# Layer-norm normalisations moved from VectorE to ScalarE in a two-layer model kernel, with new orders on four engines

## The reference: what is computed

```python
h = _L0_tok_ref(x, L0_tok_W, L0_tok_b)
h = jnp.concatenate([h, txt], axis=1)
h = h + _L0_attn_ref(_layernorm(h, axis=-1))          # plain attention, no projections
h = h + _L0_ffn_ref(_layernorm(h, axis=-1), ...)      # router takes the better half of the tokens, gelu
h = h + _L1_attn_ref(_layernorm(h, axis=-1), ...)     # 16 query heads, 1 key head, rotary, window 128
h = h + _L1_ffn_ref(_layernorm(h, axis=-1), ...)      # 32 experts, the best one for each token, relu

def _layernorm(x, axis=-1, eps=1e-05):
    m = jnp.mean(x, axis=axis, keepdims=True)
    v = jnp.var(x, axis=axis, keepdims=True)
    return (x - m) / jnp.sqrt(v + eps)
```

## Time and profile before

| | |
|---|---|
| median of three runs | 582.66 us (579.9 to 582.99) |
| the profiled execution | 583.62 us, its span in the trace 581.8 us, mean granted clock 0.971 |
| PE busy | 502.2 us (86%) |
| weight loads of PE | 386.4 us (66%) |
| DVE busy | 417.8 us (72%) |
| ScalarE busy | 311.9 us (54%) |
| GpSimd busy | 234.7 us (40%) |
| starts of hC | 148.97, 209.70, 270.42, 332.37, 394.34, 452.97, 508.66, 556.86 us |

### The profile page before, as it was taken

How to read it: one execution, slowest core, us unless ns; L and a number is a source line. 1 busy time by engine, 2 the same in 40 slices (tenths; PEclk the granted TensorE clock), 3 DMA queues, 4 the chain that set the end, 5 groups by cost and what they waited for, 6 DMA issues and landing times.

```text
span 581.8 us, 14569 instructions
## 1 busy us (share of the span) xinstructions
PE 502.2 (86%) x5920; PEld 386.4 (66%) x5920; DVE 417.8 (72%) x1291; ACT 311.9 (54%) x593; POOL 234.7 (40%) x217
## 2 busy tenths in 40 slices
PE   3457499879999899989998999899989999899845
PEld 2235277658867786778776877688767767777622
DVE  3669766996799769976997699957995697363220
ACT  1414346565667556766577565756575655454311
POOL 2316632554446342643454436354462446420000
PEclk9999999989999999999998999899999999999966
DMA  7000000000000000000000000000000000000000
GB/s 271 1 6 0 1 7 2 3 1 7 3 2 10 7 2 2 10 7 3 2 9 3 2 3 2 8 3 2 3 10 2 2 2 9 2 3 9 2 1 7
DMA packets 6450, 6.29 MB, mean 11 GB/s; under 512 B 4208, under 2 KB 5744, under 8 KB 6256
## 3 DMA queue, kind: packets, MB, share of 16 engines
q1 hardware_dynamic: 6384, 5.37, 3.0%
HBM read 4.31 MB, written 0.79 MB: 9 GB/s over the span
## 4 chain that ended last, share of the span: by engine, by line
PE 47%; DVE 35%; ACT 9%; POOL 2%; issue 2%; DMA 2%; SPq 1%; POOLq 0%; ACTq 0%; DVEq 0%
PE bank L961 38%; PE bank L979 10%; DVE eq L515 5%; DVE negm L631 4%; DVE q_sb L568 4%; DVE ssq L585 4%; DVE tb L568 4%; DVE on L648 3%; ACT qT L810 3%; POOL qs L793 2%; DMA p<-masks 2%; DVE eq L506 1%; ACT qs L810 1%; DVE eq L431 1%; DVE rec L644 1%
## 5 line engine op out<-in xcount | busy, mean ns | idle before, releaser
L631 DVE TENSOR_REDUCE negm<-bank 128x2 f32<-128x384 f32 (+1 forms) x128 | 79.2, 619 | 39.6 <-PE bank L961 38.4
L793 POOL TENSOR_TENSOR qs<-q_sb,qs 128x1024 fp32r<-128x1024 f32 x24 | 56.8, 2368 | 107.8 <-ACT qs L810 107.8
L919 ACT ACTIVATE p<-bank 128x512 f32<-128x512 f32 x112 | 66.0, 599 | 56.6 <-PE bank L961 55.4
L961 PE MATMUL bank<-kh,qT 128*128 128x128 f32 (+1 forms) x384 | 82.0, 323 | 0.0
L810 ACT ACTIVATE qT<-bank 128x512 fp32r<-128x512 f32 x96 | 54.3, 596 | 50.3 <-PE bank L979 49.9
L961 PE MATMUL bank<-vx,p 128*64 128x65 f32 x1536 | 68.8, 225 | 1.3 <-DVE on L648 1.2
L961 PEld LDWEIGHTS bank<-vx,p 128*64 128x64 f32 x1536 | 60.5, 138 | 13.9 <-issue 6.8
L756 POOL TENSOR_TENSOR q_sb<-q_sb,tb 128x512 f32<-128x512 f32 x24 | 36.5, 1519 | 74.3 <-DVE tb L568 74.3
L961 PEld LDWEIGHTS bank<-kh,qT 128*128 128x128 f32 x384 | 64.2, 199 | 2.1
L961 PE MATMUL bank<-sh_r,sh_l 128*128 128x512 f32 x112 | 53.2, 475 | 0.0
L644 DVE RECIPROCAL rec<-bank 128x4 f32<-128x4 f32 (+1 forms) x88 | 15.7, 179 | 48.4 <-PE bank L961 48.0
(11 more groups left out here) (158 smaller groups left out, 1122.9 us busy)
## 6 DMA issues: line engine op xcount, KB each, us to landing
wts<-weights SPq DMA_DIRECT2D x1, 1313.5 KB, 7.3
h<-txt SPq DMA_DIRECT2D x1, 672.0 KB, 8.4
img<-images SPq DMA_DIRECT2D x8, 72.0 KB, 1.9
q_sb<-wqkv SPq DMA_DIRECT2D x1, 576.0 KB, 9.7
sh_r<-mT SPq DMA_DIRECT2D x32, 4.0 KB
out<-o_sb SPq DMA_DIRECT2D x8, 64.0 KB, 1.9
p<-masks SPq DMA_DIRECT2D x1, 480.0 KB, 10.4
cst<-shapes SPq DMA_DIRECT2D x1, 304.0 KB, 3.8
```

The costliest lines, as they stand in the source:

```text
L631: ve.tensor_reduce(dst, src, AX_X, ALU.max, negate=True).then_inc(s_vec, 1)
L793: gp.tensor_tensor(qs[:, :, D:2 * D], ta[:, t, 0:NH, :], qs[:, :, 0:D].bitcast(F32), ALU.subtract).then_inc(b_pool, 1)
L919: ac.activation(dst.rearrange("s h t -> s (h t)"), bank[BANK_E[n % 2]][:, :], ACT.Exp).then_inc(e_act, 1)
L961: return pe.matmul(dst, lhsT, rhs, start=start, stop=stop, skip_group_check=True)
```

## The change

Nine of the eleven instructions of DVE that normalise A's two norms and D's norm become ScalarE activations (Identity, scale column `rs`, bias column `nm`), since (x - m) r = r x + (-m r). The two that write `xpad` stay on DVE, and so does B's norm. GpSimd makes the bias: it negates the means ahead of `rstd`, and multiplies them with the finished `rs` behind it. PE's transposes and GpSimd's `hx` wait for ScalarE's semaphore instead of DVE's, `ctx` on PE waits for `xpad` too. The first norm of a pair on GpSimd waits for xn2 of the pair before, as nmA is one buffer.

```diff
-A_VEC = [..., "sums1", "stats1", "xn1", "recip", "ctx", "sums2", "stats2", "xn2", "wcol", ...]
-A_POOL = ["var1", "rstd1", "var2", "rstd2", "hx"]
+A_VEC = [..., "sums1", "stats1", "pad", "recip", "ctx", "sums2", "stats2", "wcol", ...]
+A_POOL = ["var1", "rstd1", "shift1", "var2", "rstd2", "shift2", "hx"]
...
 def a_xn1(p):                                                  # DVE
     ve.wait_ge(a_pool, after(A_POOL, p, "rstd1"))
-    normalise(xa, h0[:, p.n, :, :], mvA, rsA, None)
     for b in range(2):
...
-def a_xn2(p):                                                  # DVE
-    ve.wait_ge(a_pool, after(A_POOL, p, "rstd2"))
-    normalise(xf, h0[:, p.n, :, :], mvA, rsA, a_vec)
...
-def d_xt(p):                                                   # DVE
-    ve.wait_ge(stored[p.par], p.half * (16 * OUT_DMAS))
-    ve.wait_ge(d_pool, after(D_POOL, p, "rstd"))
-    normalise(o_sb[p.par], hC, mvD, rsD, d_vec)
...
+def shift(nm, mv, rs, sem_pool, names, p, rstd_name):          # GpSimd
+    gp.wait_ge(sem_pool, after(names, p, rstd_name))
+    gp.tensor_tensor(nm[:, :], nm[:, :], rs[:, :], ALU.mult).then_inc(sem_pool, 1)
...
 def a_ln1(p):                                                  # GpSimd
     gp.wait_ge(a_vec, after(A_VEC, p, "stats1"))
+    if p.n > 0:
+        gp.wait_ge(a_act, after(A_ACT, p, "xn2") - len(A_ACT))
+    gp.tensor_tensor(nmA[:, :], mvA[:, :, 0], minus_one[:, :], ALU.mult)
     rstd(mvA, rsA, a_pool, A_POOL, p, "var1")
+    shift(nmA, mvA, rsA, a_pool, A_POOL, p, "rstd1")
...
 def a_hx(p):
-    gp.wait_ge(a_vec, after(A_VEC, p, "xn2"))
+    gp.wait_ge(a_act, after(A_ACT, p, "xn2"))
...
+def normalise(dst, src, rs, nm, done):                         # ScalarE
+    for t in range(NT):
+        ins = ac.activation(dst[:, t, 0:D], src[:, t, :], ACT.Identity, scale=rs[:, t:t + 1], bias=nm[:, t:t + 1])
+    ins.then_inc(done, 1)
...
+def d_xn(p):                                                   # ScalarE, step D:ln
+    ac.wait_ge(stored[p.par], p.half * (16 * OUT_DMAS))
+    ac.wait_ge(d_pool, after(D_POOL, p, "shift"))
+    normalise(o_sb[p.par], hC, rsD, nmD, d_act)
...
 def a_xt(src, wait, name):                                     # PE
-        wait_apart(pe, a_vec, after(A_VEC, p, wait))
+        wait_apart(pe, a_act, after(A_ACT, p, wait))
 def d_xt(p):
-    wait_apart(pe, d_vec, after(D_VEC, p, "xn"))
+    wait_apart(pe, d_act, after(D_ACT, p, "xn"))
```

More of the change, by code:

```diff
@@ L55 @@
 WEIGHT_AT, WEIGHT_N = offsets(WEIGHT_COLS)
-A_VEC = ["grid", "tok", "sums1", "stats1", "xn1", "recip", "ctx", "sums2", "stats2", "xn2", "wcol", "equal", "rank", "wsel",
+A_VEC = ["grid", "tok", "sums1", "stats1", "pad", "recip", "ctx", "sums2", "stats2", "wcol", "equal", "rank", "wsel",
          "y", "yw", "h"]
-A_POOL = ["var1", "rstd1", "var2", "rstd2", "hx"]
+A_POOL = ["var1", "rstd1", "shift1", "var2", "rstd2", "shift2", "hx"]
 A_PE = ["rows", "cols", "tok", "xT1", "s01", "s2", "ctx", "xT2", "route", "h1a", "h1b", "y"]
-A_ACT = ["rows", "xT1", "p01", "p2", "xT2", "route", "h1a", "h1b"]
+A_ACT = ["rows", "xn1", "xT1", "p01", "p2", "xn2", "xT2", "route", "h1a", "h1b"]
 B_VEC = (["sums", "stats", "xn", "hi", "xs", "r00", "r01", "ssq00", "r10", "ssq01", "r11", "ssq10", "r20", "ssq11",
@@ L69 @@
     + [f"tq{t}{i}" for t in range(NT) for i in range(4)]
-D_VEC = ["h", "sums", "stats", "xn", "logits", "top", "index", "indexf", "onehot", "off", "out"]
-D_POOL = ["var", "rstd"]
+D_VEC = ["h", "sums", "stats", "logits", "top", "index", "indexf", "onehot", "off", "out"]
+D_POOL = ["var", "rstd", "shift"]
 D_PE = ["y0", "y1", "y2", "xT", "logits", "oneT", "h0", "h1", "h2", "h3", "out"]
-D_ACT = ["xT", "oneT", "h0", "h1", "h2", "h3"]
+D_ACT = ["xn", "xT", "oneT", "h0", "h1", "h2", "h3"]
 NV = 11
@@ L233, in early_fusion @@
         rsA = sb("rsA", [P, NT])
+        minus_one, nmA, nmD = sb("minus_one", [P, NT]), sb("nmA", [P, NT]), sb("nmD", [P, NT])
         xa = sb("xa", [P, NT, D + 1])
@@ L702, in _ @@
                 ("W", "eye"): w_eye, ("W", "mask"): w_mask, ("W", "wq"): w_wq, ("A", "cols"): a_cols, ("A", "tok"): a_tok,
-                ("A", "ln1"): a_ln1, ("A", "xn1"): a_xn1, ("A", "ctx"): a_ctx, ("A", "ln2"): a_ln2, ("A", "xn2"): a_xn2,
+                ("A", "ln1"): a_ln1, ("A", "xn1"): a_xn1, ("A", "ctx"): a_ctx, ("A", "ln2"): a_ln2,
                 ("A", "rank1"): a_rank1, ("A", "rank2"): a_rank2, ("A", "rank3"): a_rank3, ("A", "y"): a_y, ("A", "h"): a_h,
@@ L709, in _ @@
                 **{("C", f"V{v}"): c_v(v) for v in range(NV)},
-                ("C", "wo2"): d_wo, ("D", "ln"): d_ln, ("D", "xT"): d_xt, ("D", "logits"): d_logits, ("D", "pick"): d_pick,
+                ("C", "wo2"): d_wo, ("D", "ln"): d_ln, ("D", "logits"): d_logits, ("D", "pick"): d_pick,
                 ("D", "out"): d_out})
@@ L722, in _ @@
             gp.memset(ln_eps[:, :], LN_EPS)
+            gp.memset(minus_one[:, :], -1.0)
             gp.memset(minus_half[:, :], -0.5).then_inc(set_pool, 1)
@@ L736, in rstd @@
                 gp.tensor_tensor(rs[:, :], rs[:, :], minus_half[:, :], ALU.pow).then_inc(sem_pool, 1)
+            def shift(nm, mv, rs, sem_pool, names, p, rstd_name):
+                gp.wait_ge(sem_pool, after(names, p, rstd_name))
+                gp.tensor_tensor(nm[:, :], nm[:, :], rs[:, :], ALU.mult).then_inc(sem_pool, 1)
             def a_ln1(p):
                 gp.wait_ge(a_vec, after(A_VEC, p, "stats1"))
+                if p.n > 0:
+                    gp.wait_ge(a_act, after(A_ACT, p, "xn2") - len(A_ACT))
+                gp.tensor_tensor(nmA[:, :], mvA[:, :, 0], minus_one[:, :], ALU.mult)
                 rstd(mvA, rsA, a_pool, A_POOL, p, "var1")
+                shift(nmA, mvA, rsA, a_pool, A_POOL, p, "rstd1")
             def a_ln2(p):
                 gp.wait_ge(a_vec, after(A_VEC, p, "stats2"))
+                gp.tensor_tensor(nmA[:, :], mvA[:, :, 0], minus_one[:, :], ALU.mult)
                 rstd(mvA, rsA, a_pool, A_POOL, p, "var2")
+                shift(nmA, mvA, rsA, a_pool, A_POOL, p, "rstd2")
             def a_hx(p):
-                gp.wait_ge(a_vec, after(A_VEC, p, "xn2"))
+                gp.wait_ge(a_act, after(A_ACT, p, "xn2"))
                 gp.tensor_tensor(hx[:, :, :], h0[:, p.n, :, :], xf[:, :, :], ALU.add).then_inc(a_pool, 1)
@@ L798, in d_ln @@
                 gp.wait_ge(d_vec, after(D_VEC, p, "stats"))
+                gp.tensor_tensor(nmD[:, :], mvD[:, :, 0], minus_one[:, :], ALU.mult)
                 rstd(mvD, rsD, d_pool, D_POOL, p, "var")
+                shift(nmD, mvD, rsD, d_pool, D_POOL, p, "rstd")
             run_program(MERGE["gp"], {**{("W", f"shr{k}"): w_shr(k) for k in range(3)}, ("A", "ln1"): a_ln1, ("A", "ln2"): a_ln2, ("A", "xn2"): a_hx, ("B", "ln"): b_ln,
@@ L822, in _, with a_xn, f @@
             bA, bD, bO = bank[BANK_A], bank[BANK_D], bank[BANK_O]
+            def normalise(dst, src, rs, nm, done):
+                for t in range(NT):
+                    ins = ac.activation(dst[:, t, 0:D], src[:, t, :], ACT.Identity, scale=rs[:, t:t + 1], bias=nm[:, t:t + 1])
+                ins.then_inc(done, 1)
+            def a_xn(dst, k):
+                def f(p):
+                    ac.wait_ge(a_pool, after(A_POOL, p, f"shift{k}"))
+                    if k == 1 and p.n > 0:
+                        ac.wait_ge(a_vec, p.n * len(A_VEC))
+                    if k == 2 and p.n > 0:
+                        ac.wait_ge(a_pool, p.n * len(A_POOL))
+                    normalise(dst, h0[:, p.n, :, :], rsA, nmA, a_act)
+                return f
+            def d_xn(p):
+                ac.wait_ge(stored[p.par], p.half * (16 * OUT_DMAS))
+                ac.wait_ge(d_pool, after(D_POOL, p, "shift"))
+                normalise(o_sb[p.par], hC, rsD, nmD, d_act)
             def a_do(name, dst, src, func=ACT.Copy, **kw):
@@ L941, in _ @@
                 ("A", "rows"): a_do(["rows"], z_sb, bA[0:IMG, 0:2 * 32]),
+                ("A", "xn1"): a_xn(xa, 1), ("A", "xn2"): a_xn(xf, 2), ("D", "ln"): d_xn,
                 ("A", "xT1"): a_do(["xT1"], xaT[0:D, :], bA[0:D, 0:PT]),
@@ L1034, in a_ctx @@
                 pe.wait_ge(a_act, after(A_ACT, p, "p2"))
+                pe.wait_ge(a_vec, after(A_VEC, p, "pad"))
                 w = D + 1
```

## The result

The changed kernel takes 584.23 us (median of 20 runs, 580.78 to 585.73), the kernel before 582.16 in as many runs beside it (579.38 to 584.54): a ratio of 1.0037, 95% interval 1.0019 to 1.0055. By the bound of 0.5% that is no change, though the interval leaves out 1: if anything the changed kernel is slightly slower. The forecast was 583.5. The profiled execution took 585.26 us with a span of 583.5, 1.7 more than before.

What follows compares the result with a forecast made beforehand. PE was taken as the bound, so only work it waits for counts. Pair 1's xn2 +0.4, pair 0's attention -3.9, five steady pairs +3.5 and last pair +0.8 gave +0.8 on 582.66: 583.5 us, range 573 to 591.

Steps and rivals of the forecast that it cites:

- the stall moves from X2 to V7: Steady pairs: rank2 still runs beside m0 and m1, so PE waits 2.3 us at V7; a pair loses 0.4.
- The start: Pair 1's xn2 (+0.4) and pair 0's attention (-3.9) together, put at -3.5 us.
- DVE's nine instructions are worth only what they take from the waits: DVE gives up 2.3 us a pair, 18 us in all, nearly all of it beside PE work.
- Three activations take 1.0 us, each 395 ns: ScalarE's normalisations: 1.0 us for three (bounds 0.64 and 1.2), against 0.76 on DVE, with 29 table loads as before.
- Last pair +0.8: Last pair's layer norm: the way from statistics to transposes, whole on the path, grows by 0.8 us (0.4 to 1.0).
- The D norm costs 0.9 a pair: Steady pairs: D:ln delays tq12, tq13, hi2 and lo2, so PE waits 0.9 us a pair (0.6 to 1.2).
- Small waits -0.6 a pair: Steady pairs: PE's small waits for a reduction of S, D:h0 and tok get other work in front, -0.6 us a pair.
- Pair 1's xn2: PE's 7.8 us wait: transposes about 2 us earlier, but hi, lo, tq end the stage; net +0.4 (-3 to +1).
- Pair 0's attention -3.9: Waits for V7 and xf go with two low-clock stretches, less new waits at V9 and tq10: -3.9 us (-7 to -1).
- Clock drops as before (two): Steady pairs: PE's clock falls as often as before, in two of five pairs, 1.2 us each.
- The faster rival: Stalls go if V6 precedes rank2 or rank2 misses m0 and m1: 570.5 us, half of it 576; chance 0.30.
- The slower rival: V7's longer wait drops the clock in every pair, with slower activations and small waits staying: 590.6 us; chance 0.33.

Runs made afterwards that it cites:

- run 1: Changed kernel's new orders of PE, DVE, GpSimd and ScalarE, but all eleven normalisations on DVE as before: 586.52 us, ratio 1.0103 to the kernel before.
- run 5: Changed kernel, orders untouched, GpSimd holding m0 of pairs 2 to 6 back until the next pair's rank2 is over: 573.41 us, ratio 0.9849 to before.
- run 3: Changed kernel with rank2 of pairs 3 to 7 moved behind V7 on DVE: 575.82 us, ratio 0.9912 to the kernel before.
- run 9: Changed kernel with DVE's old local order (V6, rank2, V7, kk) in steady pairs, PE's new order kept: 579.26 us, ratio 0.9953 to before.
- Run 7: run 3 with D's norm back on DVE in all pairs, its GpSimd shift left out: 574.52 us, ratio 0.9876 to the kernel before.

## Why the prediction was right, point by point

The time, its sign and the main mechanism came out: the stall moves from X2 to V7 and isn't removed. That the sum came so close is luck in part. The start was put at -3.5 and gave 0, the steady pairs with what follows them at +3.5 and cost 1.7, the end at +0.8 and cost 0.1; these errors nearly cancel.

- *DVE's nine instructions are worth only what they take from the waits*: right. DVE's 2.3 us a pair were worth 0.2 in a steady pair (run 1). In pair 0's attention they were worth some 4 us (run 1), and there too by a wait, that for xf.
- *Three activations take 1.0 us, each 395 ns*: 1.10 and 432 to 435 measured. By an estimate from the figures of the Trainium skill (ScalarE: Activation LUTs, What ACT_TABLE_LOAD costs) it would be 425 and 1.09; the trace agrees within 10 ns. The 213 ns that the prediction started from were a copy from PSUM on 64 partitions; no row here tells which of the two makes the 37 ns. The table loads stayed 29.
- *Last pair +0.8*: +0.75, right.
- *The stall moves from X2 to V7*: right, and runs 5, 3 and 9 show the cause. Its size was predicted at 2.3 and is 1.84 (1.44 in the first of the five), as PE stood at V7 at 312.25, which is rms + 4.1 instead of 3.65. The rule that the prediction took from the Trainium skill (SBUF — State Buffer, Who interferes with whom) agrees with the rows: the instructions with two SBUF inputs (rank2, in run 3 kk's subtraction) grow beside the multiplies, and `on`, one of whose inputs is in PSUM, keeps its 0.42. That issue order decides who blocks agrees too: a comparison that starts behind a multiply ends with it (306.78 to 308.84 in the kernel before, beside m0 until 308.63), and m0, which starts while the first comparison still runs, takes 2.09 instead of 1.90.
- *The D norm costs 0.9 a pair*: right in sum at best, and not by the wait that it named. lo2 ended 8.4 behind the start of hC (8.7 predicted), and PE reached tq20 at 280.12 by itself, 8.6 behind hC against 7.4 before. So PE doesn't wait for lo2 in a clean period. Of the wait only 0.44 is visible, at D:xT. Run 7 doesn't confirm it as a price: on DVE the same norm costs as much.
- *Small waits -0.6 a pair*: this step failed. The wait for `negm` stays at 0.3, and waits of 0.36 for `xsT` and 0.2 for `mT` are new; those for D:h0's and `tok`'s inputs, 0.2 each, did go. With stall and D norm smaller and this gain missing, a clean period came to +0.45 where +0.7 was predicted.
- *Pair 1's xn2*: PE waits 6.7 instead of 7.8, and tq20 of pair 0 begins at 92.42 instead of 92.61. -0.2 where +0.4 was predicted, inside its bounds: lo2 is what ends the stage. The 7.8 had a part that the prediction didn't name: xn2's three instructions, which have one tensor input from SBUF, took 2.59 in the kernel before, and not 0.76; the third of them took 1.94, beside m0. DVE's timeline:

```profile
60.92 2.59 DVE L454 TENSOR_SCALAR xf<-h,mvA,rsA 128x64 f32<-128x64 f32 x3
```

- *Pair 0's attention -3.9*: this step failed as a gain of the whole. X2 came 3.5 us earlier (125.16 against 128.66), the wait for xf fell from 1.55 to 0.23, and the two low-clock stretches (6.8 us together) went. But a new one, as long, came at 94 to 101 us, V9 waited 1.4 and tq10 0.56 (1.6 and 0.9 predicted), and PE waited for `xaT` and `negm` in the next stage besides: at tq20 of pair 1 the gain was 0. The step took what PE gains up to X2 for a gain of the whole; the stage behind, and the clock ahead of it, were not looked at.
- *Clock drops as before (two)*: one in the steady pairs, worth 1.5 (62.67 against 61.17); run 3 and run 5 have none there. In the sum, the start gave 3.5 us less than predicted (0 for -3.5), and the five steady periods, pair 5's extra and the drop less took 1.8 less (1.7 for +3.5), with the end at +0.1 for +0.8; so the spans' +1.7 stands where +0.8 was predicted.
- Of what the profile was to show if the forecast was right, periods of 61.4 or 62.6 came as 61.17 and 62.67, waits at V7 as 1.84. X2 of pair 0 came 3.5 us earlier, where about 5 stood.

The faster rival, "the stalls do go", has its price about confirmed: by their ratios runs 3 and 5 would be 577.0 and 573.4 beside a before of 582.16, where 570.5 to 576 stood. Its condition (V6 reaches DVE before rank2, or rank2 doesn't meet m0 and m1) is what the change doesn't meet. The slower rival didn't come, since the clock fell behind one of the five waits at V7, where it had fallen behind two of the five at X2. What decides it isn't shown.

What stays open: what starts the low clock at 94 to 101 us, and pair 5's 1.3 us, of which only 0.9 are waits that the trace names.

## What to carry to other kernels

Look at which instructions run beside each other before you move work off an engine: here 3.3 us of DVE's 5.0 were its neighbour's. One wait on GpSimd made the kernel before 1.3% faster, 1.9% with pair 1 included. Nine instructions moved off DVE, with new orders for them, gave nothing. A new order that leaves the colliding pair together only chooses who pays. Where a hand-written order and an offload come in one change, time each with the other undone: the offload alone costs 2.6% at the better of two places for D:ln, the orders alone 1.0%, both together 0.4%.
